# Reordering the eight dense sequences of a scan-plus-routed-experts layer, and giving the first of them an opening of its own

## The reference

```
xn  = layernorm(x)
g, v, d = xn @ Wg + bg, xn @ Wv + bv, xn @ Wd + bd          # each 256 wide
attn = linear_scan(sigmoid(g) * tanh(v), decay = 0.001 + 0.998 * sigmoid(d))   # along the sequence
scores = sigmoid(xn @ Wr.T + biases)                        # 8 experts
top_scores, top_idx = top_k(scores, 2)
combined[t] = sum over its two experts e of top_scores * (gelu(xn[t] @ W1[e].T + b1[e]) @ W2[e].T + b2[e])
shared = gelu(xn @ Ws1.T + bs1) @ Ws2.T + bs2               # 256 -> 1024 -> 256
out = x + attn + shared + combined
```

## Time and profile before

| | us |
|---|---|
| median of 3 runs (737.7, 738.0, 742.22) | 738.0 |
| the profiled execution's own time | 739.86 |
| its span in the profile | 737.6 |
| mean granted TensorE clock | 0.984 |

### The profile page before, as it was taken

How to read it: one execution, slowest core, us unless ns; L and a number is a source line. 1 busy time by engine, 2 the same in 40 slices (tenths; PEclk the granted TensorE clock), 3 DMA queues, 4 the chain that set the end, 5 groups by cost and what they waited for, 6 DMA issues and landing times. The chain is left out here.

```text
span 737.6 us, 20181 instructions
## 1 busy us (share of the span) xinstructions
PE 666.5 (90%) x5816; PEld 517.8 (70%) x5817; DVE 525.4 (71%) x1381; ACT 432.3 (59%) x738; POOL 305.1 (41%) x261
## 2 busy tenths in 40 slices
PE   2689898999999998889999999999999999998784
PEld 1246555555656474568888888888889888887663
DVE  4579797988889898866666667666666676675542
ACT  6766858686777766435555555555555555554542
POOL 2015251524333343315455456446446545544321
PEclk9899999999999999999999999999999999999998
DMA  7307171716152624113233234233333334333231
GB/s 268 143 11 154 65 161 42 172 29 170 36 164 36 164 58 115 44 44 57 58 64 57 58 64 64 52 62 64 56 58 65 56 61 68 52 56 53 51 53 15
DMA packets 54170, 57.53 MB, mean 78 GB/s; under 512 B 13204, under 2 KB 48916, under 8 KB 54136
## 3 DMA queue, kind: packets, MB, share of 16 engines
q1 hardware_dynamic: 38456, 38.42, 20.4%
q0 software_dynamic: 15680, 18.69, 16.0%
HBM read 38.53 MB, written 18.55 MB: 77 GB/s over the span
## 5 line engine op out<-in xcount | busy, mean ns | idle before, releaser
L1098 PE MATMUL bank<-W,arena 128*128 (+1 forms) x2304 | 304.7, 274 | 20.4 <-DVE arena L821 17.4
L1090 PE MATMUL bank<-rows,W 128*128 128x256 f16 (+1 forms) x1920 | 301.8, 295 | 4.4 <-issue 3.3
L1098 PEld LDWEIGHTS bank<-W,arena 128*128 128x128 f16 x2304 | 221.4, 98 | 64.8 <-DVE arena L821 27.7
L1090 PEld LDWEIGHTS bank<-rows,W 128*128 (+1 forms) x1920 | 186.6, 99 | 59.4 <-issue 4.5
L464 POOL DMA_INDIRECT out<-arena,slot_add x71 | 120.5, 1697 | 180.6 <-ACT arena L647 170.9
L545 ACT ACTIVATE arena<-bank,par 128x256 f32<-128x256 f32 x256 | 134.3, 560 | 83.3 <-PE bank L1090 78.2
L820 DVE TENSOR_SCALAR arena<-arena,par 128x256 f16<-128x256 f32 x284 | 102.7, 362 | 78.7 <-ACT arena L545 49.3
L821 DVE SCALAR_TENSOR_TENSOR arena<-arena,par 128x256 f16<-128x256 f32 x284 | 138.7, 488 | 10.1
L419 POOL DMA_INDIRECT lists<-entry,place x64 | 80.7, 1261 | 119.5 <-DVE entry L817 102.4
L453 POOL DMA_INDIRECT rows<-xhl_rows,slot_list x71 | 77.7, 1094 | 52.9 <-DMA slot_list<-lists 26.9
L1078 PE MATMUL bank<-rows,W 128*128 128x512 f16 x288 | 67.5, 394 | 6.2 <-ACT arena L531 6.2
(11 more groups left out here) (152 smaller groups left out, 528.9 us busy)
## 6 DMA issues: line engine op xcount, KB each, us to landing
stage<-in_w SPq DMA_DIRECT2D x32, 512.0 KB, 7.0
b2row<-in_b SPq DMA_DIRECT2D x39, 128.0 KB
arena<-in_x SPq DMA_DIRECT2D x8, 512.0 KB
xhl_rows<-W SPq DMA_DIRECT2D x8, 512.0 KB
out<-arena SPq DMA_DIRECT2D x8, 512.0 KB
W<-in_w SPq DMA_DIRECT2D x4, 512.0 KB, 8.4
rows<-xhl_rows,slot_list POOLq DMA_INDIRECT x71
out<-arena,slot_add POOLq DMA_INDIRECT x71
```

The lines of the kernel that those rows point to most:

```text
L1090: ins = T.matmul(bank_, weights(w, wp * HALF + c * H + j * P, P), rhs[:, 2 * xp + c, :], start=n == 0, stop=n == 3 * KD - 1)
L1098: ins = T.matmul(banks[t // 2][:, (t % 2) * D:(t % 2 + 1) * D], h[:, hp, t * P:(t + 1) * P], weights(w, (2 + wp) * HALF + j * D, D), start ...
```

## The change

No operation of the slots changes. In the sequences the orders of PE, ACT and DVE change, `scales` becomes shorter, and the first sequence gets queues of its own (`opening`) on ACT and DVE. The new matrix product `norm_sum` takes two matmuls in place of one, and adds the two parts of each layer in PSUM; it writes a corner of the bank that holds the logits and ranks, and therefore waits for `place_ok`. POOL fills the entries ahead of the scatter, not behind it. PE multiplies a tile of ones, `WARM` = 24 times after the first norm sum and 12 times after the turn of x. The last weights' squares are written to places that are free earlier. The diff, cut to what sets the order:

```diff
@@ PE
-            def x_transposes(b, i):
+            def x_transposes(b, i, to=ps_t16):
...
-                T.matmul(sums[:, 0:4], onesf[:, :], ssq, start=True, stop=True).then_inc(norm_ok, 1)
+                halves = ssq.rearrange("p (l q) -> p l q", q=2)
+                for part in range(2):
+                    ins = T.matmul(sums, onesf[:, :], halves[:, :, part], start=part == 0, stop=part == 1)
+                ins.then_inc(norm_ok, 1)
...
-                    if k == (2 if last_ else PROJ):
+                    if k == (2 if last_ else PROJ - 1):
                         ranks(b)
-                    if k == 2 and first:
-                        norm_sum(0, ps_y[0])
+                    if k == 1 and first:
+                        norm_sum(0, ps_y[0][:, 0:2])
...
-                    if i == 0 and not last_:
-                        pe.wait_ge(xT_ok, b * 2 + 2)
-                        norm_sum(b + 1, ps_t)
+                    if i == (4 if first else 2 if last_ else 0):
+                        pe.wait_ge(place_ok, b + 1)
+                        norm_sum(b + 1, ps_l[:, 128:130])
+                    if i == 1:
+                        pe.wait_ge(scan_ok, b * 2 + 2)
+                        scan_transposes(b, 0)
                     if i == 2:
-                        pe.wait_ge(scan_ok, b * 2 + 2)
-                        pe.wait_ge(scale_ok, b + 2 if last_ else b + 3)
-                        scan_transposes(b, 0)
-                        if last_:
-                            norm_sum(NW - 1, ps_l)
-                    if i == 3:
                         pe.wait_ge(r_ok, b * 2 + 1)
                         scan_transposes(b, 1)
-                    if i == 5 and not last_:
+                    if i == 4 + first and not last_:
...
-                    if i == 6 and not last_:
+                    if i == 5 + first and not last_:
...
-            norm_sum(-1, ps_y[0])
+            norm_sum(-1, ps_y[0][:, 0:2])
+            for i in range(WARM):
+                T.matmul(ps_e[2][:, 0:P], ones[:, :], ones[:, :], start=True, stop=True)
+            pe.wait_ge(xhi_ok, 1)
+            x_transposes(0, 0)
             pe.wait_ge(xhl_ok, 1)
-            x_transposes(0, 0)
-            pe.wait_ge(xT_ok, 1)
-            x_transposes(0, 1)
+            x_transposes(0, 1, ps_low16)
+            for i in range(WARM // 2):
+                T.matmul(ps_e[2][:, 0:P], ones[:, :], ones[:, :], start=True, stop=True)
@@ ACT
+            def opening():
+                for i in range(2):
+                    projection(0, 0, i)
+                for part in range(2):
+                    high_part(0, 0, part)
+                projection(0, 0, 2)
+                decay(0, 0)
+                projection(0, 0, 3)
+                projection(0, 0, 4)
+                high_part(0, 1, 0)
+                projection(0, 0, 5)
+                high_part(0, 1, 1)
+                gelu_wide(0, 0, 0)
+                decay(0, 1)
+                score(0)
+                squares(1, 0, 0)
...
             def sequence(b, u, last_=False):
                 for i in range(PROJ):
                     projection(b, u, i)
                     if i in (2, 5):
                         decay(b, i // 3)
-                    if i == 2 and last_:
+                    if i == 1:
+                        squares(b + 1, 0, 0)
+                    if i == 4:
                         score(b)
-                    if not last_:
-                        if i == 1:
-                            squares(b + 1, 0, 0)
-                        if i >= 3:
-                            squares(b + 1, (i - 2) // 2, (i - 2) % 2)
+                        squares(b + 1, 0, 1)
...
                 for i in range(KH):
                     gelu_wide(b, u, i)
+                    if i in ((1, 2) if last_ else (0, 1)):
+                        squares(b + 1, 1, i - last_)
-                    if i == 0:
+                    if i == 1 and not last_:
                         normed(b + 1, 1 - u)
-                    if i == 1:
+                    if i == 2 and not last_:
                         act.wait_ge(xhl_out, b * 16 + 16)
                         x_high(b + 1)
...
-            for part in range(4):
-                high_part(0, part // 2, part % 2)
             act.wait_ge(bias_half, 1)
             act.wait_ge(spare_out, 64)
-            sequence(0, 0)
+            opening()
@@ DVE
+            def opening():
+                for part in range(5):
+                    best_two(0, part)
+                variances(1, 1)
+                scales(0)
+                for part in range(2):
+                    low_part(0, 0, part)
+                scan_input(0, 0)
+                scan(0, 0)
+                for part in range(2):
+                    low_part(0, 1, part)
+                scan_input(0, 1)
+                split_wide(0, 0)
...
+                split_wide(0, 4)
+                scales(1)
+                x_low(1)
+                split_wide(0, 5)
+                low_part(1, 0, 0)
+                split_wide(0, 6)
+                low_part(1, 0, 1)
+                split_wide(0, 7)
+                add_bias(1, 1)
...
                 if last_:
                     for part in range(5):
                         best_two(b, part)
...
+                if last_:
+                    places(b, u)
...
                 for i in range(KH):
                     split_wide(b, i)
                     if i == 0:
+                        if not last_:
+                            places(b, u)
                         scan(b, 1)
-                    if i == 3 and not first:
-                        dve.wait_ge(o_out, b * 16)
-                    if i in (3, 4):
-                        residual(b, u, i - 3)
-                    if last_:
-                        if i < 3:
-                            tables(i)
-                        if i == 4:
-                            scales(NW - 1)
...
+                    if i == 1 and not last_:
+                        scales(b + 1)
+                    if i == 3 and last_:
+                        scales(b + 1)
                     if i == 2:
-                        places(b, u)
-                        x_low(b + 1)
-                    if i in (5, 7):
-                        low_part(b + 1, 0, (i - 5) // 2)
+                        if not last_:
+                            x_low(b + 1)
+                        dve.wait_ge(o_out, b * 16)
+                    if i in (2, 3):
+                        residual(b, u, i - 2)
+                    if last_ and i in (1, 2, 4):
+                        tables((1, 2, 4).index(i))
+                    if i == 4 and not last_:
+                        low_part(b + 1, 0, 0)
+                    if last_ and i >= 5:
+                        low_part(b + 1, (i - 5) // 2, (i - 5) % 2)
...
                 else:
                     add_bias(b + 1, 1 - u)
+                    low_part(b + 1, 0, 1)
```

More of the change, by code:

```diff
@@ L52 @@
 EXPONENT = 0x7F800000
+SMALLEST = float(48 << 23)
 EPS = 1e-5
@@ L58 @@
 WIDE = 2
+WARM = 24
 EVENTS = PROJ + KH
@@ L516, in x_T @@
                 act.wait_ge(xT_ps, b * 2 + i + 1)
-                A(xT[u][:, 2 * i:2 * i + 2, :], chunks(ps_t16, 2), ACT.Copy).then_inc(xT_ok, 1)
+                turned = ps_low16 if isinstance(b, int) and (b, i) == (0, 1) else ps_t16
+                A(xT[u][:, 2 * i:2 * i + 2, :], chunks(turned, 2), ACT.Copy).then_inc(xT_ok, 1)
             def score(b):
@@ L837, in sequence @@
                         best_two(b, part)
-                if not first:
-                    for part in range(2):
-                        low_part(b, 1, part)
-                    shared_result(b - 1, 0)
-                    shared_result(b - 1, 1)
+                for part in range(2):
+                    low_part(b, 1, part)
+                if last_:
+                    places(b, u)
+                shared_result(b - 1, 0)
+                shared_result(b - 1, 1)
                 if not last_:
@@ L967, in _ @@
             V.engine_nop().then_inc(bias_half, 1)
-            scales(0)
-            for part in range(4):
-                low_part(0, part // 2, part % 2)
-            dve.wait_ge(bs2_in, 16)
-            add_bias(0, 0)
-            sequence(0, 0, first=True)
+            opening()
             sequence(1, 1)
@@ L1207, in sequence @@
                         first_layer(0, j, 0, w)
+                    for part in range(2):
+                        pe.wait_ge(stage_used[1][part], NW)
             pe.nop().then_inc(scanT_ps, 2)
```

116 lines of the change are left out of this document (61 added, 55 removed).

## The result

| | before | after |
|---|---|---|
| median of 20 runs each, us | 741.38 (735.92 to 743.87) | 743.39 (741.09 to 746.29) |
| the profiled execution, its span | 739.86, 737.6 | 742.4, 740.6 |
| mean granted TensorE clock | 0.984 | 0.979 |

The ratio of the runs is 1.0041, with a 95% interval of 1.0025 to 1.0058: no gain but 0.4% more, where 727 was forecast. The chip of these runs isn't on record. On a chip numbered 10 the same changed kernel later took 725.33, with a ratio of 0.9797. Most of this text is about that difference.

The account below looks back on a forecast made before the run. PE was taken as the floor in sequences 1 to 6, DVE close under it. Opening -3.5, middle -10.2 and last sequence +2.1 sum to -11.6 us, giving 727 us; range 716 to 736, own range 722 to 731.

Parts of the forecast that it names:

- up to logits(1): Opening: earlier logits, scales and first eviction, half given back at expert 1's norm sum; -3.5 us, bounds -7 and 0.
- sequences 1 to 6: Middle: about 33.5 us a sequence instead of 35.3, -1.7 each, -10.2 us in all.
- from logits(7) to the end: Last sequence: later tables delay route_ok by about 6.7 us, less 4.4 slack; taken as +2.1 us, bounds 0 and +4.
- Link three: what is late next: Middle: last splits wait for PE, +0.8 instead of 0.24, so link two's gain shrinks from 1.4 to about 0.65 us.
- list of new waits: PE's norm sum waits some 0.4 us, covered by chunk 1's split; second matmul covered; weight loads and POOL's fill cost nothing.
- the 1.35: Link two, DVE's scales in each sequence: 8 steps, four waited for, take 1.35 us instead of 2.77.
- the 13.65 of link three: Middle: PE finishes layer 2 of chunk 4, which split 6 needs, 13.65 us after the first split.
- The rival in which PE becomes the only bound: Link three's waits don't bite: middle -17, last sequence 0, opening -5, about 716 us; chance 0.17.
- the one in which the loop re-closes: Work ahead of split 1 holds PE like the old waits: middle -4, opening -2, last +2, about 734 us; chance 0.30.
- the fallen clock: Opening: after PE's idle time ahead of chunk 5, a fallen clock adds up to 1 us before sequence 1 starts.
- The ones: Opening: matmuls of ones cost nothing beside PE's idle time and are worth 0 to 0.5 us through the clock.
- The slower one: Late squares hold the norm sum in PE's queue: 3 us a sequence, 18 in all, about 745 us; chance 0.08.

Follow-up runs that it names:

- after_again: The changed kernel run again unchanged on chip 10, beside the kernel before: 725.33 us against 739.44, ratio 0.9797.
- a_noscatter: The changed kernel without POOL's list scatters of sequences 2 to 5, DVE's loop kept, on chip 13: 727.02 us, ratio 0.9823.
- a_unrolled: The changed kernel with DVE's loop over sequences 2 to 5 written out, on chip 13: 726.86 us, ratio 0.981.
- a_unr_tables: The changed kernel, DVE's loop written out, first sequence's scatters held until its residuals are written, last sequence's tables and scales placed as before: 721.42 us, ratio 0.9761.
- a_spaced: The changed kernel, loop kept, with POOL's scatters meant to go out in pairs behind splits 1 to 4, on chip 8: 725.88 us, ratio 0.9842.
- a_resid_late: The changed kernel with scan transposes and residuals of sequences 1 to 6 one chunk later, on chip 13: 742.62 us, ratio 1.0026.
- a_unr_tables_2: a_unr_tables run again beside the changed kernel on chip 10: 722.74 us, ratio 0.9758 to the kernel before.

## Why the prediction was wrong

By terms, in us against the kernel before's own trace; the middle column is the profiled run of the result, the last that of after_again.

| term | forecast | after | after_again |
|---|---|---|---|
| up to logits(1) | -3.5 | -0.34 | -1.90 |
| sequences 1 to 6 | -10.2 | +3.79 | -12.03 |
| from logits(7) to the end | +2.1 | -0.45 | +0.83 |
| sum | -11.6 | +3.0 | -13.1 |

**The step that failed** is "Link three: what is late next", with the list of new waits behind it. It gave every handover between engines no time at all. Where DVE's queue was shortened, I asked which instruction it would wait for, and added +0.8 for layer 2. I went over the waits that the change adds on PE and found them covered, rightly: PE's norm sum (L1096) shows no idle time in sequence 2. I didn't ask what DVE's wait for `scanT_ps` would meet in its new place, one chunk earlier and with a shorter queue ahead of it. It met POOL's scatters. The prediction has no term for them: it priced only the fill ahead of them, at nothing. The price was 4 x 4.1 us, and 2.6 more in the opening. a_noscatter and a_unrolled each give the middle back: 134.63 and 132.86 from logits 2 to 6, where my 33.5 a sequence makes 134.0. Why the update is late only with scatters, DVE's loop and some chips together stays open.

**The mechanism of the middle was right** where updates aren't held. after_again has 33.7 a sequence in the loop (forecast 33.5) and 31.7 and 33.2 outside it, and its sequence 4 (161.77 to 195.44) shows the links, PE and then DVE:

```profile
176.99 1.48 PE L1151 MATMUL bank<-W,arena 128*128 128x256 f16 x12 [1.14 <-DVE arena L844]
...
180.26 0.15 DVE L727 TENSOR_SCALAR small<-bank 128x2 int32<-128x2 int32 x1
...
181.85 0.48 DVE L843 TENSOR_SCALAR arena<-arena,PT 128x512 f16<-128x512 f32 x1
...
190.82 0.49 DVE L843 TENSOR_SCALAR arena<-arena,PT 128x512 f16<-128x512 f32 x1 [0.41 <-PE bank L1151]
...
192.58 0.48 DVE L843 TENSOR_SCALAR arena<-arena,PT 128x512 f16<-128x512 f32 x1 [0.48 <-PE bank L1151]
```

PE waits 1.14 at chunk 0 (forecast 1.1), DVE waits 0.89 for PE at chunks 6 and 7 (0.8), and PE doesn't wait before the next logits. From the first step of the scales to the split it takes 1.59, not 1.35; four steps of 0.2 and four of 0.08 to 0.1 make 1.2 at most, so the 1.35 doesn't follow from its own terms. Nor do the 13.65 of link three, whose terms make 12.95. The -12.03 is more than the -10.2 because sequence 1 alone fell from 35.9 to 31.7, which no term had. That the sum of after_again, -13.1, lies near the -11.6 is in part luck: the middle and the end came out better by 1.8 and 1.3, the opening worse by 1.6.

The rival in which PE becomes the only bound (-17) and the one in which the loop re-closes (-4) both miss.

**Opening.** The steps came out one by one: logits at 14.94 (15.0), the idle PE ahead of chunk 5 at 3.65 in after_again (3.8). Two sizes were off. The first eviction came at 26.24, not 25.1: the packets of zeros were not done at 25, since 7 of the 82 that started in 25 to 25.5 were still of 2 KB and more, and 2 in the next half us; the last landing that `spare_out` counts is recorded at 26.17. And the fallen clock, "up to 1", took more: behind that idle time three groups of PE take 2.74, 1.06 and 2.63 us, that take 1.48, 0.61 and 1.47 further on, 2.9 us in all. That, too, was one execution: sequence 1 starts at 62.74 there, and between 61.31 and 63.27 over the traces of the changed kernel and its variants on the three chips, where 61.1 was forecast. With the late update (6.24 us idle instead of 3.65) only 0.34 of the 3.5 was left.

**The ones**: the first units ran at the upper clock at once, and the 26.24 that everything waits for is `spare_out`'s. Both agree with the forecast, without a run that leaves the ones out.

**Last sequence.** `route_ok` came 30.3 us after the logits (31.0), PE stood 4.04 us ahead of the rows ("about 4"), and logits to slot 0 took 42.4 (43.2, before 41.14). Of the delay of `route_ok`, 6.7 us in the forecast, the terms given (1.4 and 5.0) make only 6.4. But the slots were 1.7 us shorter, 418.60 for 420.29, and the term counted the tables only: a_unr_tables shows that it was worth undoing.

**The rivals.** The slower one named late squares as its mechanism. They didn't occur, and its price, 3 us a sequence, was near the real one for another reason. No rival was a handover that comes late, and the kernel before's own trace had shown them: its layer 2 behind the second transposes of the scan ends at 201.38 in sequence 4 and its update is recorded at 201.90, without anyone waiting. The range, 716 to 736, holds the 725.33 of chip 10 and not the 743.39 of the result.

## What to carry to other kernels

When a change moves a cross-engine wait, ask not only when the producer is done but what else is being issued there: here a wait that cost nothing before fell into a burst of indirect DMAs and cost 4 us each time. Look for the end of the producer's instruction against the start of the waiting one; "remote" as releaser, with the producer long done, is its mark. Before an experiment is read against another, run the kernel in question beside it on the same chip: four tests here could show nothing of the hold because it wasn't there, and the ratio of the change itself turned from 1.004 to 0.980. And read from the trace that an edit did what it was to do: the scatters of a_spaced never parted.

## What the runs showed of the hardware

- TensorE's semaphore updates, usually recorded 0.01 to 0.02 us behind the matmul's modelled end, came up to 4.75 us late while GpSimd gave out indirect DMAs 0.96 us long and 0.30 apart. Those that DVE waited for in the changed kernel came 1.15 to 1.32 us after the last DMA of the burst had ended; one in a_resid_late came while they still ran. The Trainium skill, page "Perfetto Trace Analysis", section "Tensor Engine Instruction (MATMUL, LD_WEIGHTS)", lists such a step, the spreading of the update after PSUM's acknowledgement, without a duration. That the delay arises in this step is not shown.
- It is a matter of the chip or its condition, or of the recording: 110 to 139 late or unrecorded updates of 841 in six traces, 1 in each of the fourteen traces of chips 8, 10 and 15. In the slots updates are recorded mostly 0.3 to 1.3 us late around the scatter-adds as well, but it cost nothing there: the slots took 418.6 us with it and 419.5 without (after_again). The kernel before had medians of 741.38 and 742.14 us beside kernels with late updates, and of 737.65 to 739.44 on chips 8, 10 and 15.
- A loop on VectorE cost the changed kernel some 0.4 us a sequence against the written-out form even without late updates: 33.66 in after_again and 33.21 in a_unr_tables_2, both on chip 10.
